# Graph convolution: a fifth chunk of source columns a turn, evenly shared copies, and attribute loads issued by SyncE

## What is computed

```python
h = jnp.maximum(_layernorm(x, axis=-1), 0.0)
filters = jax.nn.silu(edge_attr @ fW1 + fb1) @ fW2 + fb2      # 206250 x 50 -> 128 -> 128
messages = (h[src] @ dW + db) * filters
aggregated = jax.ops.segment_sum(messages, dst, num_segments=6250)
x = x + jax.nn.silu(aggregated @ uW1 + ub1) @ uW2 + ub2
```

## Time and profile before

| | us |
|---|---|
| median of 3 runs (lowest, highest) | 5505.33 (5501.94, 5513.48) |
| the profiled execution's own time | 5491.89 |
| its span, first to last instruction | 5490.1 |

### The profile page before, as it was taken

The page is one execution under the profiler, slowest core; times in us unless marked ns, Lnnn a source line. Parts: engine busy times, 40 slices in busy tenths (PEclk is TensorE's granted clock), DMA queues, the critical chain, the costliest instruction groups (busy, mean ns, idle before and its releaser), DMA issues. The chain is left out here.

```text
span 5490.1 us, 88496 instructions
## 1 busy us (share of the span) xinstructions
PE 3661.5 (67%) x14349; PEld 2797.4 (51%) x14350; DVE 3149.1 (57%) x13756; ACT 2573.3 (47%) x14407; POOL 2913.4 (53%) x3066
## 2 busy tenths in 40 slices
PE   4666666566565666665656777767777767777777
PEld 2444444444444444444445556555555555565556
DVE  5666666666565666666644555555555554555554
ACT  4333434343343334433414555555555555555554
POOL 5555555555555555555545555545555555555553
PEclk6555555555555555555556556666566666656666
DMA  4112122121111112122132122121221211212211
GB/s 102 45 45 47 45 46 48 46 47 45 45 45 45 45 45 47 45 46 46 45 95 56 52 55 56 51 54 51 54 55 52 55 53 53 55 51 55 56 52 45
DMA packets 192455, 284.64 MB, mean 52 GB/s; under 512 B 84692, under 2 KB 137403, under 8 KB 187704
## 3 DMA queue, kind: packets, MB, share of 16 engines
q0 software_dynamic: 97088, 202.29, 15.3%
q1 hardware_dynamic: 90408, 40.70, 2.9%
q10 hardware_dynamic: 4840, 40.55, 2.4%
HBM read 264.60 MB, written 15.70 MB: 51 GB/s over the span
## 5 line engine op out<-in xcount | busy, mean ns | idle before, releaser
L63 POOL DMA_INDIRECT ae_xg<-table,ae_idx x1592 | 1506.0, 946 | 1188.1 <-issue 488.6
L63 POOL DMA_INDIRECT ce_xg<-table,ce_idx x1442 | 1368.2, 949 | 1282.7 <-DVE ce_msg L1797 806.6
L1634 ACT COPY ce_held<-sums 128x4 uint8 x11008 | 1232.6, 190 | 1013.2 <-issue 1003.5
L1761 DVE COPY ce_held<-sums 128x4 uint8 x8256 | 752.2, 184 | 631.5 <-issue 629.1
L1700 PE MATMUL ce_ps_h<-ce_ea,ce_fw 50*128 50x384 f32 x1076 | 661.6, 757 | 570.3 <-ACT ce_hid L1618 421.4
L1158 PE MATMUL ae_ps_k<-ae_xg,ae_e 128*96 128x129 f32 x3224 | 888.9, 433 | 6.9 <-remote 6.8
L1158 PEld LDWEIGHTS ae_ps_k<-ae_xg,ae_e 128*96 128x96 f32 x3224 | 685.8, 276 | 146.6 <-issue 120.6
L1669 PE MATMUL ce_ring<-ce_fw,ce_hid 128*128 128x128 f32 x3228 | 702.5, 402 | 1.9 <-issue 1.7
L1669 PEld LDWEIGHTS ce_ring<-ce_fw,ce_hid 128*128 128x128 f32 x3228 | 661.9, 309 | 60.6 <-issue 59.4
L1700 PEld LDWEIGHTS ce_ps_h<-ce_ea,ce_fw 50*128 50x128 f32 x1076 | 265.4, 272 | 732.9 <-ACT ce_hid L1618 360.1
L1678 PEld LDWEIGHTS ce_ring<-ce_hot,ce_msg 128*128 128x128 f32 x3224 | 537.0, 255 | 35.9 <-issue 35.8
(11 more groups left out here) (193 smaller groups left out, 4094.5 us busy)
## 6 DMA issues: line engine op xcount, KB each, us to landing
ce_stage<-table SPq DMA_DIRECT2D x2688, 0.5 KB
ae_stage<-table SPq DMA_DIRECT2D x2560, 0.5 KB
ce_ea<-in_edge_attr ACTq DMA_DIRECT2D x88, 450.0 KB
ae_xg<-table,ae_idx POOLq DMA_INDIRECT x1592
ce_xg<-table,ce_idx POOLq DMA_INDIRECT x1442
sums<-in_x SPq DMA_DIRECT2D x7, 448.0 KB, 4.8
sums<-features SPq DMA_DIRECT2D x1, 3136.0 KB
table<-sums SPq DMA_DIRECT2D x6, 462.0 KB, 3.8
```

The source lines that it names most:

```text
L63: eng.indirect_dma_start(out=out, out_offset=None, in_=table[:, :], in_offset=bass.IndirectOffsetOnAxis(ap=idx, axis=0)).then_inc(done, 16)
L1634: one = nc.scalar.copy(held_bytes[:, 4 * (m * P + k):4 * (m * P + k) + 4], by_byte[:, bass.ds(start, 4)])
L1761: one = nc.vector.tensor_copy(held_bytes[:, 4 * (m * P + k):4 * (m * P + k) + 4], by_byte[:, bass.ds(start, 4)])
```

## The change

Five edits, all in the convolution.

A fifth column chunk, the sixth chunk of slot 1, is added to `COLUMNS`, and each column is shared evenly; GpSimd skips that chunk too, since it goes by `TO` (31 gathers a turn). Both engines make 48 copies in every slot, 288 a turn; VectorE's second piece becomes 32 copies, read in two portions. The address lists are laid out in four rows of `columns` (partitions 0, 32, 64 and 96) for three, filled by four DMAs. The attribute loads of the next turn are issued by SyncE, in `load_beside` directly behind the index load, after a wait for the half's third `s_hid`; the loads of `y` in turn 0 come behind them. The two `head_slot` numbers are changed.

```diff
-    with nc.Fori(OPEN + 1, SHUT, engines=[engine], hint_back_edge=True, head_slot={engine: 140}) as i:
+    with nc.Fori(OPEN + 1, SHUT, engines=[engine], hint_back_edge=True, head_slot={engine: 105}) as i:
...
-COLUMNS = (Column(0, 3, False, 55, 73), Column(2, 5, False, 55, 73), Column(3, 1, True, 55, 73), Column(CARRY_SLOT, 2, True, 27, 37))
+COLUMNS = (Column(0, 3, False, 64, 64), Column(1, 4, False, 64, 64), Column(2, 5, False, 64, 64), Column(3, 1, True, 64, 64), Column(CARRY_SLOT, 2, True, 32, 32))
...
-SCALAR = Share([48, 40, 40] * 2, [range(c.vector, c.count) for c in COLUMNS])
-VECTOR = Share([2 * READ] * SL, [range(c.vector) for c in COLUMNS])
+SCALAR = Share([48] * SL, [range(c.vector, c.count) for c in COLUMNS])
+VECTOR = Share([48] * SL, [range(c.vector) for c in COLUMNS])
...
-    with nc.Fori(2, TURNS - 1, engines=[engine], hint_back_edge=True, head_slot={engine: 160}) as i:
+    with nc.Fori(2, TURNS - 1, engines=[engine], hint_back_edge=True, head_slot={engine: 45}) as i:
...
-            ahead(r, i + 1, v)
+            following(r, i, v)
+            results(r, i, v)
             if v == 0:
                 beside(r, i)
...
-                if isinstance(i, int) and i == 1:
+
+            def following_attributes(r, i, v):
+
+                sp.wait_ge(s_hid, r * UNITS + i * SL + (v + 1) * LOAD + XS)
+                sp.dma_start(ea[:, v, :],
+                             a["edge_attr_50"][:, 0:10, bass.ds(((i + 1) * LOADS + v) * LOAD * UE, LOAD * UE)]).then_inc(ea_in[v], 16)
+
+            def results(r, i, v):
+
+                if isinstance(i, int) and i == 0:
                     for g in range(v * (GROUPS - 1) // LOADS, (v + 1) * (GROUPS - 1) // LOADS):
                         sp.dma_start(y[:, g, :, :], sent[g * GN:(g + 1) * GN, :].rearrange("(t p) f -> p t f", p=P)).then_inc(y_in, 16)
...
-                        if s % LOAD == LOAD - 1 and not (isinstance(i, int) and i == TURNS - 1):
-                            following_attributes(i, s // LOAD)
...
-                    part = VECTOR.slot(s)[piece * READ:(piece + 1) * READ]
+                    part = VECTOR.slot(s)[READ:] if piece else VECTOR.slot(s)[:READ]
```

More of the change, by code:

```diff
@@ L868, in collect, with load_beside @@
                 sp.dma_start(self.stage[p:p + 1, b, :].bitcast(u8), self.bytes[:, bass.ds(start, size)]).then_inc(self.rows_in, 16)
[L871 removed]
+def load_beside(nc, sp, a, h, idx, idx_in, gathered, landed, rows, xg, xg_free, ahead, following, results, beside, listed):
     def read(r, i, v, count=SL):
@@ L1538, in convolution_edges @@
         drawn = sb("drawn", [COLUMN_TURNS, SCALAR.total + VECTOR.total], i32)
-        columns = sb("columns", [65, COLUMN_TURNS * VECTOR.total], i32)
-        half = SCALAR.start(SL // 2)
-        by_row = [drawn[:, 0:half], drawn[:, half:SCALAR.total], drawn[:, SCALAR.total:]]
+        by_half = [list(zip((share.start(0), share.start(LOAD)), (share.start(LOAD), share.total))) for share in (SCALAR, VECTOR)]
+        columns = sb("columns", [97, COLUMN_TURNS * max(b - a for ends in by_half for a, b in ends)], i32)
+        in_half = [ends[0][1] for ends in by_half]
+        assert all(b - a == width for ends, width in zip(by_half, in_half) for a, b in ends)
         held = sb("held", [P, len(COLUMNS), P])
```

21 lines of the change are left out of this document (10 added, 11 removed).

## The result

The changed kernel takes 5546.57 us (median of 5 runs, 5532.01 to 5550.0), the kernel before in the same comparison 5505.33 us (5 runs, 5496.62 to 5520.86): ratio 1.0065, interval 1.0043 to 1.0088. It is slower, as forecast, by 41 us where 104 were forecast. The profiled execution has a span of 5530.2 us against 5490.1.

A forecast was written before the change was run, and what follows sets the result against it. ScalarE was taken to bound the kernel at 9.89 us a unit; 9.89 + 0.82 - 0.30 - 0.12 = 10.29, over 258 units +103 us, +0.6 at the start, gave a median of 5609 us, range 5460 to 5705.

The forecast's parts named there:

- ScalarE's copies: ScalarE in the convolution: 5.33 more copies a unit cost 0.82 us, between 0.54 at full pace and 1.09 at mean price.
- What bounds the kernel now: Convolution turns: ScalarE sets the pace at 9.89 us a unit, waiting for nobody; VectorE has 1.93 us a unit of slack.
- ScalarE's attribute issues: ScalarE's queue: losing two attribute load issues a turn saves 0.30 us a unit of "issue" before the SiLU.
- The gather saved: GpSimd, 31 gathers a turn for 32: credits ScalarE 0.12 us a unit of held-up time, bounds nothing to 0.21.
- VectorE: Sixteen more copies and a third address read add 2.34 us a unit; occupied time goes from 7.96 to 10.27, slack gone.
- The 10.29 for both engines: Convolution unit after the change: ScalarE at 10.29 us and VectorE at 10.27, so the two stand level.
- rival 4: SyncE's late issues set the pace: 62.3 us a turn, +129 us, 5634 us, with late attribute loads and indices; chance 0.08.
- Rival 3: VectorE alone sets the pace at 10.8 us a unit: +194 to +235 us, 5700 to 5740; chance 0.10.
- rival 1: Added copies cost full pace only, ScalarE deciding at 9.92 to 9.98 us a unit: +8 to +25 us, about 5525; chance 0.15.
- SyncE: Issuing both attribute loads in the convolution costs nothing, with half a microsecond a turn to spare.
- Rival 2: Attribute loads from SyncE shield copies from gathers: faster, 5435 us, or 5470 with half the gain; chance 0.25.
- The start: Before the convolution: a fourth load of the column lists delays TensorE's first attributes by 0.6 us.

The follow-up runs named there:

- Four even: Kernel before, its four chunks' copies shared evenly, 37.33 a unit per engine: 5314.56 us, ratio 0.9756 where held up; 3923.69 us, 1.0014 on a free chip.
- one gather less: Kernel before, sixth chunk of slot 1 not gathered from turn 2 on and nothing in its place: 5376.48 us, ratio 0.9847.
- columns only: The changed kernel, but ScalarE issues the attribute loads as before: 5454.34 us, ratio 0.9982 to the kernel before.

## Why the prediction was right in sign and too large

The kernel got slower by 41 us where 104 were forecast. My sum went by ScalarE, which was to rise from 9.89 to 10.29 us a unit; it fell to 9.75. VectorE, which was to come to 10.27, came to 10.06 and sets the time. Two terms were mis-sized, ScalarE's copies and VectorE's, and since I had the engines level it takes both to get from the forecast to the result.

By halves the forecast was further off than the sum shows. My terms for the columns alone, with the loads left on ScalarE, give 9.89 + 0.82 - 0.12 = 10.59 us a unit, +3.3%; the run has 1800 / 183 = 9.84 us and a ratio of 0.998. For the move of the loads I had -0.30 us a unit, -1.4%; by the ratios of two chips it cost 0.8%. So two errors of opposite sign partly cancel, and that the sign of the whole came right is in part luck.

- **What bounds the kernel now: right**, where engines are held up. Four even gained 2.4% by relieving ScalarE alone. On a free chip it would have been wrong: GpSimd paces there, which a trace of a held-up chip, with 570.5 us of waits on GpSimd, can't show.
- **ScalarE's copies: the step that failed in the sum that I went by.** "I take the middle, 0.82: some will fall into bursts, but bursts don't become more." Together with the gather's share (-0.12) that was +0.70 us a unit. Measured: (869.5 + 717.9) / 182 = 8.72 us a unit for the copies before, (955.2 + 638.3) / 179 = 8.90 after, +0.18. The copies' busy time rose by 5.34 - 4.78 = 0.56 us, the full pace (0.54). The "issue" before them, for which I had +0.28 with the copies and -0.12 with the gather, fell from 710.3 / 182 = 3.90 to 628.8 / 179 = 3.51 us. It is 0.735 us per gather before (710.3 / 966) and 0.682 after (628.8 / 922); with four even it is 0.673 (655.9 / 975). More copies don't catch more of it. So an added ScalarE copy is worth its full pace of 0.10 us at most, and the half-price for held-up time had no ground. On one chip the step from one gather less to columns only says the same: 0.30 us a unit for what I had at 0.82. The second half of my own sentence said so and I did not follow it to its number. With 0.54 the sum is 9.89 + 0.54 - 0.30 - 0.12 = 10.01, against 9.75 to 9.86 found. Mended alone, this step would have left the forecast where it was, at VectorE's 10.27.
- **ScalarE's attribute issues: right.** The "issue" before the SiLU, 53.9 us, is gone from the row of L1624; -0.30 us a unit. It bought no time: the columns-only run has it still (69.8 us at L1624) and a unit of 9.84 us.
- **The gather saved: too small, it seems.** I credited 0.12 us a unit. One gather less in the kernel before gave 1.5%, 84 us or 0.33 us a unit; one more in the changed kernel cost 0.3%, within its interval. On a free chip, where GpSimd paces, it is worth the 0.9% of the run with VectorE's copies thinned out.
- **VectorE: right that its slack goes; the term that sets the time, 0.21 us too much.** I had 7.96 + 2.34 + 0.05 - 0.08 = 10.27 us; it is 10.06, a rise of 2.10 for 2.31. Of the 62 us that the forecast was over, 258 x 0.21 = 54 lie here. The composition was off as well. I had 1.24 us for the copies at full pace and 1.10 for the third read. VectorE as a whole is busy for 948.0 us of the 1800 before and 1214.4 after, 5.21 and 6.78 us a unit: +1.57, for the copies and the fifth placing, where I had 1.29. The "issue" before its copies went from 439.3 / 182 = 2.41 to 540.7 / 179 = 3.02 us: +0.61, for hold-ups and the third read together, where I had 1.10 - 0.08. So the busy time came 0.28 us dearer than I had it, and the term put too high is the 1.10 us for the read. Unlike on ScalarE, this idle time grew with the copies; how much of it is hold-up and how much the read, no run separates there. On the free chip an open read has less to hide in: VectorE's occupied time went from 6.67 - 1.19 (its waits) = 5.48 to 7.10 - 0.07 = 7.03 us, +1.55, its copies with the idle time before them from 3.18 to 4.66, +1.48, and the "issue" in that from 102.8 / 195 = 0.53 to 121.8 / 183 = 0.67. So the third read cost 0.14 us at most there, not 1.10: it goes ahead while the engine works off its queue. Reads aren't free all the same: the chain of the kernel after has L505 with 5% of the span.
- **The 10.29 for both engines.** My sum had them level; they are 0.2 to 0.3 us apart, with VectorE the pace and ScalarE waiting 0.31 us a unit. Rival 3 had the mechanism (VectorE alone), at a price of 10.8 us that was far off; rival 1 had ScalarE's price nearly, and its time, 5525, was closer than mine.
- **SyncE: right that it is covered in the change, wrong on why and by how much.** I had it half a microsecond a turn ahead; it waits 6.0 us before each load. Its issue takes 0.79 us, not 1.26, the wait at L883 (3.0 us a turn) is gone, and 32 row loads take 19.4 us on average, not 23.1. But the move by itself, at the kernel before's shares, is rival 4: 2.8%, by late indices.
- **Rival 2, attribute loads that shield copies: not settled.** Between columns only and the change the ratio rises by 0.8%, and VectorE is held up more. That is the reverse of the gain it named; but the two are of different chips, and no run moved the moment of the loads alone.
- **The start: right in size.** TensorE's wait for the first attributes went from 29.3 us to 31.7 us: +2.4 where I had 0.6, too small to matter.
- **What the hold-ups are: open.** I tied them to the gathers because they start and end with their bursts. The gathers run on free chips too, 1.25 us apart, and hold up little: a ScalarE copy costs 0.106 us there and 0.204 here. So I take the gathers for the occasion, while something of the chip decides the price; no run here tells what, and the runs meant to tell by spacing or pairing the gathers all fell on free chips.

## What to carry to other kernels

Before pricing added work on an engine that often stands in "issue", ask what that idle time goes with. If it goes with other traffic (here about 0.7 us per gather), an added instruction can cost its full pace alone, as ScalarE's did, and not the mean that includes the idle time; check it for each engine, since VectorE's idle time did grow. And a slack read on one chip is that chip's: the same change cost 0.65% where engines were held up and 2.8% where they were not, because the engine that paced before was another. The share that beat both kernels where engines are held up (2.4%) and lost 0.14% elsewhere was the plain one: the same copies as before, evenly divided.

## What the runs showed of the hardware that I had not expected

- The same kernel took 3918 to 3925 us on two chips and 5465 to 5543 us on the others. The stage ahead of the convolution is longer too: the first read of L505 starts at 2901.0 us, and at 2153.8 us in the run of four even on a free chip. On the slow kind ScalarE and VectorE pass one instruction every 0.71 us for stretches of several, at the same instants (4204.00 to 4206.12 above), and at other places one every 1.4 us, as SyncE does with its row loads then; on the fast kind a ScalarE copy costs 0.106 us on average, on the slow one 0.204.
- A read of addresses into registers has a price by where it starts: 16 words in 1.02 us from a multiple of 16 bytes, 3.44 us from others; 23 words 2.05 and 5.15 us. The Trainium skill, Runtime: NRT & Kernel Launch, Instruction fetch mechanics, gives some 200 ns a register for a load of registers from HBM; these addresses come from a tile in SBUF. The slow reads are near that figure (5.15 / 23 = 0.22 us a register), the quick ones (1.02 / 16 = 0.064) far below. Two copies a unit moved from one engine to the other, with the reads cut to fit, took the ratio from 0.998 to 1.129 by this, as far as the traces show.
